# A two-layer conditioned transformer block on one core: a third chunk ahead of the feed-forward stage, a new written order, and more weight splitting on GpSimd

## The reference

```python
# L0: masked attention, RMS norm of its output, shift and scale from cond
q, k, v = (proj(Wq), proj(Wk), proj(Wv))
scores = jnp.where(mask[None, None, :, :], -jnp.inf, scores)
out = einsum('bhst,bhtd->bhsd', softmax(scores, axis=-1), v) @ Wo.T
xn = out / sqrt(mean(out*out) + EPS) * rms_scale
x = x + xn * (1.0 + sc[:, None, :]) + shift[:, None, :]
# L1 (its sum is added to x once more)
x1 = x + attention(tc_rmsnorm(x, t, g1w, g1b, b1w, b1b), Wq, Wk, Wv, Wo)
x = x + x1 + swiglu(tc_rmsnorm(x1, t, g2w, g2b, b2w, b2b), gate_w, hid_w, out_w)
```

## Time and profile before

| | |
|---|---|
| median of 3 runs | 336.03 us |
| profiled execution | 333.88 us |
| its span | 332.1 us |
| PE busy | 317.1 us, 95% |
| DVE busy | 238.8 us, 72% |
| ACT busy | 208.7 us, 63% |
| POOL busy | 171.8 us, 52% |
| granted TensorE clock, mean | 0.995 of full |

### The profile page before, as it was taken

The page is one execution under the profiler, slowest core; times in us unless marked ns, Lnnn a source line. Parts: engine busy times, 40 slices in busy tenths (PEclk is TensorE's granted clock), DMA queues, the critical chain, the costliest instruction groups (busy, mean ns, idle before and its releaser), DMA issues.

```text
span 332.1 us, 12175 instructions
## 1 busy us (share of the span) xinstructions
PE 317.1 (95%) x5152; PEld 299.5 (90%) x5152; DVE 238.8 (72%) x413; ACT 208.7 (63%) x449; POOL 171.8 (52%) x195
## 2 busy tenths in 40 slices
PE   5999679889999999999999999999999999999995
PEld 5878569788899999999999999999999999999995
DVE  3799855988767788698968887698598685255343
ACT  3888747979686855857598575575554653543221
POOL 7073589950352527358474657638527367144231
PEclk9999979999999999999999999999999999999999
DMA  7926642220301030001300030000001000000000
GB/s 244 261 74 196 191 130 66 80 82 4 100 2 35 2 99 2 3 2 35 97 2 34 10 92 1 2 34 2 2 2 34 5 34 0 2 28 6 2 34 32
DMA packets 11238, 17.09 MB, mean 51 GB/s; under 512 B 1328, under 2 KB 5440, under 8 KB 11184
## 3 DMA queue, kind: packets, MB, share of 16 engines
q1 hardware_dynamic: 11008, 15.80, 15.1%
q0 software_dynamic: 176, 0.51, 0.8%
HBM read 14.14 MB, written 2.16 MB: 49 GB/s over the span
## 4 chain that ended last, share of the span: by engine, by line
PE 82%; DVE 7%; issue 3%; DMA 3%; SPq 2%; ACT 1%; POOL 1%; POOLq 0%; DVEq 0%
PE ps L1565 64%; PE ps L1688 5%; PE ps L1670 5%; PE ps L1721 3%; PE ps L1706 3%; PE ps L1753 2%; DMA w_stage<-in_weights 1%; DMA mod_tile<-mod_rows_dram 1%; SPq L309 1%; DVE row_max L1127 1%; PE ps L1658 1%; DVE probs L1135 1%; PE ps L1732 1%; DVE w_lo L1115 1%; DVE in_lo L1122 1%
## 5 line engine op out<-in xcount | busy, mean ns | idle before, releaser
L1565 PE MATMUL ps<-ff_hi,w_hi 128*128 128x256 f32 x256 | 73.9, 289 | 0.0
L1565 PE MATMUL ps<-ff_hi,w_lo 128*128 128x256 f32 x256 | 72.3, 282 | 0.0
L1565 PE MATMUL ps<-ff_lo,w_hi 128*128 128x256 f32 x256 | 72.3, 282 | 0.0
L469 POOL TENSOR_TENSOR h_lo<-w_stage,h_hi 128x512 fp32r<-128x512 f32 x31 | 40.0, 1293 | 44.3 <-ACT h_hi L752 44.2
L1127 DVE TENSOR_REDUCE row_max<-ps 128x8 f32<-128x512 f32 x64 | 41.7, 681 | 15.3 <-PE ps L1670 15.2
L1565 PEld LDWEIGHTS ps<-ff_hi,w_hi 128*128 128x128 f32 x256 | 48.3, 189 | 0.9 <-issue 0.3
L1217 DVE SCALAR_TENSOR_TENSOR w_stage<-w_stage,ps 128x512 f32<-128x512 f32 x32 | 22.0, 686 | 37.1 <-ACT w_stage L745 37.0
L1565 PEld LDWEIGHTS ps<-ff_hi,w_lo 128*128 128x128 f32 x256 | 48.3, 189 | 0.0
L1565 PEld LDWEIGHTS ps<-ff_lo,w_hi 128*128 128x128 f32 x256 | 48.3, 189 | 0.0
L463 POOL TENSOR_TENSOR probs<-probs,inv_row 128x512 f32<-128x512 f32 x32 | 34.0, 1073 | 26.5 <-DVE inv_row L1148 26.3
L689 ACT ACTIVATE probs<-probs 128x512 f32<-128x512 f32 x64 | 39.1, 628 | 8.5 <-DVE probs L1135 8.3
(11 more groups left out here) (111 smaller groups left out, 824.7 us busy)
## 6 DMA issues: line engine op xcount, KB each, us to landing
w_stage<-in_weights SPq DMA_DIRECT2D x20, 256.0 KB, 4.4
mod_tile<-mod_rows_dram SPq DMA_DIRECT2D x32, 128.0 KB, 3.2
x_T<-in_xT SPq DMA_DIRECT2D x8, 256.0 KB, 3.0
x_row<-in_x SPq DMA_DIRECT2D x8, 256.0 KB, 2.8
out<-x SPq DMA_DIRECT2D x7, 256.0 KB, 2.1
x<-in_cond POOLq DMA_DIRECT2D x1, 392.0 KB, 6.3
out<-x SPq DMA_DIRECT2D x2, 128.0 KB, 1.7
x<-in_rows POOLq DMA_DIRECT2D x1, 96.0 KB, 6.3
```

The lines of the kernel that those rows point to most:

```text
L469: pool.tensor_tensor(h_lo[q % 2][:], h_T[q % 2], h_hi[q % 2][:], ALU.subtract)\
L1565: mm = pe.matmul(dst, x, y, start=first and n == 0, stop=last and n == len(terms) - 1, skip_group_check=True)
```

## The change

It rewrites the order lists of all five streams and the bank tables that go with them, and changes five things that can be named:

- `CHAINS` lets layer 0 of a fourth chunk, (3,0), go before layer 1 of the first, (0,1), and keeps that distance.
- `SWAP` goes from 8 to 6: chains 6 and 7 are weighed the second way.
- `HI_POOL` goes from 8 to 4 and `LO_DVE` from 8 to 6: POOL makes the high parts of blocks 4 to 7 in ACT's place, and the low parts of blocks 6 and 7 in DVE's.
- `LOW_DVE = 29`: the low parts of the last three hidden groups, not of the last one alone, are made on DVE.
- `gain_in` has a wait for `input_lo` or `ff_input_lo`, both on the same stream.

```diff
-LO_DVE, HI_POOL, NSTAGE = 8, 8, 5
+LO_DVE, HI_POOL, NSTAGE = 6, 4, 5
 CHAINS = [
-    (0, 0), (1, 0), (2, 0), (0, 1), (3, 0), (1, 1), (4, 0), (2, 1), (5, 0), (3, 1), (6, 0), (4, 1),
-    (7, 0), (5, 1), (6, 1), (7, 1),
+    (0, 0), (1, 0), (2, 0), (3, 0), (0, 1), (4, 0), (1, 1), (5, 0), (2, 1), (6, 0), (3, 1), (7, 0),
+    (4, 1), (5, 1), (6, 1), (7, 1),
 ]
...
-SWAP = 8
+SWAP = 6
...
+LOW_DVE = 29
...
+        def hidden_lo_of(q):
+            return (h_lo_ready, q + 1) if q < LOW_DVE else (h_lo_last, q + 1 - LOW_DVE)
...
             load_w("k0")
             load_xT(0)
-            load_xT(1)
             load_w("q0")
             load_w("v0")
             load_w("o0")
+            load_xT(1)
             load_w("k1")
...
-                wait(dve, h_lo_ready, q - 1)
+                if q >= 2:
+                    dve.wait_ge(*hidden_lo_of(q - 2))
...
-            def last_hidden_lo():
-                q = 4 * NCH - 1
+            def hidden_lo(k, g):
+                q = 4 * k + g
...
-                pe.wait_ge(h_lo_ready, q + 1)
+                pe.wait_ge(*hidden_lo_of(q))
...
-                pe.wait_ge(h_lo_last, 1)
+                pe.wait_ge(*hidden_lo_of(4 * NCH - 1))
```

More of the change, by code:

```diff
@@ L821, in _ @@
             input_hi(5)
-            input_hi(6)
+            squares_of_y(1)
+            output_hi(2)
+            exponentials(3, 2)
+            copy_keys(4)
+            copy_queries(4)
+            exponentials(3, 3)
+            copy_keys(5)
+            squares_of_x(1)
             copy_pT(3, 1, 0)
@@ L1342, in _ @@
-            shift(6, 2)
-            modulate_y(3)
-            shift(6, 3)
-            norm_output(5)
+            shift(6, 0)
+            shift(6, 1)
+            norm_x(4)
+            sums(6, 0)
+            sums(6, 1)
+            gain_in(4)
+            shift(6, 2)
+            shift(6, 3)
+            sums(6, 2)
+            norm_output(5)
+            ff_input_lo(0)
+            sums(6, 3)
+            maximum(7, 0)
+            maximum(7, 1)
+            shift(7, 0)
+            shift(7, 1)
@@ L1386, in _ @@
+            norm_x(5)
             norm_x(6)
[L1387 to L1388 removed]
+            gain_in(5)
+            gain_in(6)
+            ff_input_lo(1)
             maximum(9, 0)
+            maximum(9, 1)
             shift(9, 0)
[L1391 removed]
+            output_lo(8)
+            result(0)
+            maximum(9, 2)
+            maximum(9, 3)
             shift(9, 1)
+            input_lo(11)
+            shift(9, 2)
             sums(9, 0)
             sums(9, 1)
[L1395 removed]
@@ new lines, in _ @@
+            hidden(1, 0)
+            hidden(1, 1)
+            new_x2(2)
+            shift(9, 3)
+            modulate_y(5)
+            sums(9, 3)
+            hidden(1, 2)
+            maximum(10, 0)
+            maximum(10, 1)
+            shift(10, 0)
+            shift(10, 1)
+            norm_x(7)
+            norm_x(8)
+            sums(10, 0)
+            maximum(10, 2)
+            maximum(10, 3)
+            input_lo(12)
+            sums(10, 1)
+            gain_in(7)
+            gain_in(8)
@@ L1484, in _ @@
+            hidden(3, 0)
+            new_x2(4)
+            sums(13, 3)
+            hidden(3, 1)
             modulate_y(7)
-            hidden(3, 1)
             hidden(3, 2)
-            sums(13, 2)
-            sums(13, 3)
+            norm_x(11)
             norm_x(12)
             hidden(3, 3)
+            gain_in(11)
             gain_in(12)
+            input_lo(15)
+            result(3)
+            ff_input_lo(4)
             maximum(14, 0)
@@ L1877, in _ @@
-            hidden_in(0, 2, y_read(4), out_read(5))
-            hidden_in(0, 3)
-            output_product(5, scores_read(6, 3))
-            transpose_probs(6, 0, v_read(6), oT_read(5))
-            transpose_probs(6, 1, out_read(5), gu_read(0, 0))
-            values(7, gu_read(0, 0))
-            scores(7, gu_read(0, 1), pT_read(6, 0, 0), pT_read(6, 0, 1))
-            hidden_out(0, 0, y_read(5))
-            keys(8, pT_read(6, 1, 0))
-            queries(8, scores_read(7, 0))
-            transpose_normed(4, v_read(7))
@@ L1935, in _ @@
+            hidden_in(1, 3)
+            output_product(8, scores_read(9, 1))
+            hidden_in(1, 4, gu_read(1, 0))
+            hidden_in(1, 5)
+            transpose_probs(9, 0, y_read(8), scores_read(9, 2))
+            scores(10, gu_read(1, 1), scores_read(9, 3), y_read(7))
+            values(10, pT_read(9, 0, 0))
+            hidden_out(1, 0, gu_read(1, 2))
             hidden_out(1, 1)
             hidden_out(1, 2)
+            transpose_normed(7, v_read(10))
+            keys(11, pT_read(9, 0, 1))
@@ L1960, in _ @@
+            queries(12, pT_read(10, 0, 0))
+            transpose_probs(10, 1, pT_read(10, 0, 1), acc_read(1))
+            values(11, scores_read(11, 0))
+            output_product(9, scores_read(11, 1))
+            hidden_in(2, 0, q_read(12), pT_read(10, 1, 0))
             hidden_in(2, 1)
-            hidden_in(2, 2, xsT_read(8), scores_read(11, 1))
+            hidden_in(2, 2, scores_read(11, 2), scores_read(11, 3))
             hidden_in(2, 3)
-            keys(13, scores_read(11, 2))
-            scores(12, k_read(12), q_read(12), gu_read(2, 0))
@@ new lines, in _ @@
+            transpose_normed(10, pT_read(12, 0, 0))
+            output_product(11, oT_read(11))
+            weigh_values_T(12, pT_read(12, 1, 1))
+            scores(13, xsT_read(10), pT_read(12, 0, 1), pT_read(12, 1, 0), gu_read(2, 3))
+            values(13, gu_read(2, 3))
+            hidden_out(2, 6)
+            hidden_out(2, 7)
+            output_product(12, oT_read(12))
+            hidden_in(3, 0, scores_read(13, 0), acc_read(2))
+            hidden_in(3, 1)
+            hidden_in(3, 2, scores_read(13, 1), scores_read(13, 2))
```

1167 lines of the change are left out of this document (555 added, 612 removed), and 20 rows, old and new, of tables (GU_BANK, S_BANK, T_BANK).

## The result

The changed kernel took **325.44 us** as the median of 4 runs (324.68 to 326.48), beside 336.18 us for the kernel before on the same chip (335.86 to 338.05). The ratio is 0.967, with a 95% interval from 0.962 to 0.972: 10.7 us faster, where 6.4 were forecast. The two profiled executions are closer together, 333.88 and 326.18 us, 7.7 us apart. In all that follows the medians are over all runs of a kernel, and the ratios compare only runs within 1.5% of the fastest of their kernel.

What follows compares the result with a forecast made beforehand. PE, busy in 95% of the span, was taken as the bound. The terms -0.6 - 4.8 - 1.0 + 2.0 - 1.4 - 0.6 summed to -6.4 us: 327.5 us profiled, 329.6 us median, range 323 to 337.5 us.

Steps and rivals of the forecast that it cites:

- B: Hole from 30 to 50 us: chain-3 filler saves 7.1 us, POOL's split costs DVE 2.3 us by port contention; -4.8 us.
- A: Start: q0, v0 and o0 loaded ahead of the second x_T, the gain partly waited for again; -0.6 us.
- signs named for B: 35 to 50 us: no clock under 0.9; PE over 9 of 10 us from 30 to 50; first bias_in near 45 us.
- C: Stretch from 60 to 70 us: the order puts input_lo further ahead of its keys; -1.0 us, ends 0 and -2.1.
- D: Chains 6 and 7: SWAP adds row sums on DVE and normalise on POOL; +2.0 us, ends 0 and +7.0.
- E: Chains 6 and 7 on PE: SWAP takes 0.69 us of work off each; -1.4 us, far end 0.
- F: Tail: DVE instead of POOL makes the last low parts, removing PE's wait of 0.7 us; -0.6 us.
- Rival 1: 35 to 110 us: ACT and DVE become the pace; at worst 341.6 us; chance 0.13 slower, 0.11 within 1%.
- Rival 2: Port: five early DVE subtractions each wait for a whole POOL subtraction, 6.5 us instead of 2.3; 333.8 us; chance 0.10.
- Rival 3: Everything fits: A and C in full, B without its 2.3 us, D at nothing; -12.4 us, 323.6 us; chance 0.08.
- at nothing: Costed at no effect: four high parts leaving ACT, gain_in's added wait, and store_mods behind u1 in SP's queue.
- I apply the same difference to the median: Median taken as 2.15 us above the profiled execution before (336.03 against 333.88 us), so 327.5 became 329.6 us.

Runs made afterwards that it cites:

- second group: Four kernels made from the kernel before (split alone, new tail, first loads, extra products), on one chip beside the kernel before: 338.56 us median of its 35 runs.
- first group: Changed kernel again (326.15 us), filler taken out, split undone and SWAP = 5, on one chip beside the kernel before: 338.14 us median of its 23 runs.

## Why the prediction was right, and where it was not

The sign, the place and the bound were right; that the sum came so near is in part luck, as B shows. By profiled executions 6.4 us were forecast and 7.7 came; the median was forecast 4.2 us too high (329.6 against 325.44), inside the range.

**A** (-0.6 forecast): the first 10 us gained 1.8 us of busy PE, and 10 to 30 us gave back 0.8, so 1.0 net. The profile of the run that undoes it says 0.6. The kind of forecast, a gain that is partly waited for again, was right.

**B** (-4.8): 3.1 us of idle time and 1.7 us of clock, 4.8 us in sum. The sum was exact and its parts were not. The port contention that was to cost 2.3 us did not come where it was charged. These are the five subtractions ahead of the first maximum, with those of the earlier trace rows to compare:

```profile
9.26 0.92 DVE L1135 TENSOR_TENSOR in_lo<-x_T,in_hi 128x512 fp32r<-128x512 f32 x1 [1.26 <-ACT in_hi L668]
...
11.06 1.88 DVE L1128 TENSOR_TENSOR w_lo<-w_stage,w_hi 128x512 fp32r<-128x512 f32 x3
13.98 0.69 DVE L1135 TENSOR_TENSOR in_lo<-x_T,in_hi 128x512 fp32r<-128x512 f32 x1 [1.04 <-ACT in_hi L668]
```

They took 3.49 us, and five alone take 5 x 0.69 = 3.45. While DVE made the three `w_lo` POOL stood waiting 3.57 us for a block (from 10.66 to 14.23 us). The first maximum did come 1.4 us later (14.59 against 13.20 us), but the first exponential did not (16.50 against 16.61). In place of the contention came 1.54 us of "issue" from 33.94 us on and a wait of 0.53 us for DVE's `probs` ahead of 46.85 us. So the agreement is a cancellation. Of the signs named for B, the clock came true (1.00 in every window of 2 us from 35 to 50). PE over 9 of 10 us held from 40 to 50 us (9.20), not from 30 to 40 (8.46). And `bias_in` was expected near 45 us and ran at 47.98: I had taken the walk to shorten, and it did not.

**C** (-1.0): 50 to 70 us lost 0.4 us of idle time. The wait for `in_lo` is gone and an issue stall of 1.39 us stands there.

**D** (+2.0): from 70 us on idle time rose by 1.0 us, with none of it a wait for `normalise`. The run with `SWAP = 5` shows that the mechanism is real and starts one chain earlier.

**E** (-1.4): PE's busy time fell from 317.14 to 313.62 us, 3.5 us, of which 1.7 are the clock; the rest, 1.8, is near the 1.4 forecast. The records confirm it: 768 matmuls of L1730, 640 of L1745, and 136 fewer in all.

**F** (-0.6): -0.7; the wait for POOL's `h_lo` is gone.

**Rival 1**: from 50 to 110 us PE was idle 2.5 us in sum, half of the 5 named as its sign, and never over 1.3 us in a stretch of ten. **Rival 2**: the five subtractions above exclude it, and so do the means over the kernel, both under the 1.2 us named as its sign:

```profile
L1135 DVE TENSOR_TENSOR in_lo<-x_T,in_hi 128x512 fp32r<-128x512 f32 x8 | 7.7, 963 | 2.3 <-ACT in_hi L668 2.3
L1128 DVE TENSOR_TENSOR w_lo<-w_stage,w_hi 128x512 fp32r<-128x512 f32 x6 | 4.0, 686 | 1.1 <-ACT w_hi L654 1.1
```

The rule of the Trainium skill (SBUF — State Buffer, "SBUF: two separate sides"), that the loser of the lock waits for the other's whole instruction, is not refuted, and where the two engines met the trace agrees with it. `in_lo` took 1.62 us at 75.99 us and 1.34 us at 138.45 us, and both ended 0.54 us after the POOL instruction that they met (`new_x1`, 75.78 to 77.07 us, and `shift_row`, 137.96 to 139.25 us). The eight `in_lo` from `x_T` cost 963 ns in the mean, before 813, but these two meetings are not with the split's work. **Rival 3** (323.6 us) is nearer to the median than the forecast, but not by its terms: in the profiled pair C came to 0.4 us and D to 1.0, and the sum to 7.7, not 12.4.

**Two steps failed.** The first: "at nothing", for the high parts that leave ACT, and the port as the only effect of the split. Undoing the split in the new order costs 8.8 us. It keeps ACT and DVE free early (2.4 us of the walk) and it frees the slots in time (6.7 us of the walk, by POOL's queue), and without it the late walk stops the filler by way of ACT's `squares_of_x(0)` (6.5 us of PE's time). I had costed who does the work and not when the buffer comes free, nor what stands behind the walk. How much of the 8.8 us each of the two is worth stays open, and the run with SP's queue repaired does not settle it, since it made h2 late itself.

The second: "I apply the same difference to the median." The median is not the profiled execution plus a constant. The mean granted clock of each of 35 runs of the kernel before, in the second group:

| mean clock | runs | medians, us |
|---|---|---|
| 0.994 to 0.995 | 10 | 335.1 and 335.7 |
| 0.989 to 0.990 | 7 | 338.9 and 337.5 |
| 0.984 to 0.985 | 8 | 338.6 and 338.9 |
| 0.979 to 0.980 | 6 | 340.8 and 340.0 |
| 0.974 to 0.975 | 3 | 342.6 and 342.8 |

(Medians are given for the lower and the upper value of each pair; one run at 0.843 took 355.33 us.) A step of 0.005 is 0.005 x 332 = 1.7 us, exactly the loss read in the earlier trace rows. From 0.995 to 0.975 the time rises by about 7 us for 4 steps, 1.8 us each (1.7 by the first three rows alone). The profiled execution had one such drop, at 0.995, and was among the quickest; most runs had two to four. In the trace of the kernel with the new tail in the old order, mean clock 0.98, they can be seen:

```profile
40.00:50.00 10.00, 7.41 (x164) 6.52 (x164) 5.13 (x11) 4.07 (x12) 7.33 (x11) 0.66 0.43 125
50.00:60.00 10.00, 9.32 (x119) 9.03 (x120) 4.37 (x7) 6.50 (x18) 9.67 (x11) 0.83 0.19 56
...
70.00:80.00 10.00, 8.99 (x229) 8.53 (x230) 6.79 (x11) 6.42 (x13) 2.69 (x3) 0.83 0.18 56
```

0.34 + 0.17 + 0.17 of 10 us is 6.8 us, four times 1.7, and PE's busy time is 322.7 us there, 5.6 us more than in the profiled kernel before with its one drop (317.1). The changed kernel had a mean clock of 0.999 or 1.000 in all ten of its runs in the result and the first group. So the gain has two parts: 7.7 us in the profiled pair, with one drop in it, and the further drops that most runs of the kernel before had. That the filler is what removes the drops is shown by the run without it, whose clock fell to between 0.979 and 0.990 in all 12 runs.

The drops account for only a part of the missing 3 us. Of these, 0.7 us is the changed kernel, whose median is under its own profiled execution (325.44 and 326.18 us). The other 2.3 us is the kernel before, whose profiled execution was a quick one even for its clock: 333.88 us, where the ten runs at 0.995 in the table have 335.1 and 335.7. In the second group, 4.7 us above the profiled execution by the median, some 3 us are drops and some 1.5 the spread at one clock. What made that spread no run shows, and for the first four runs themselves no clock is on record.

## What to carry to other kernels

When a filler goes into a hole, ask not only who does each piece of work but when the piece frees its buffer, and what stands behind the loads that wait for it: moving weight parts to an idle engine was worth nothing in one order and 8.8 us in the other. Look also for what the filler's own copies stand behind: here one late step ahead of them on ACT stopped the filler for 6.5 us. A short idle hole of PE costs more than its length if the clock falls behind it, and that cost differs from run to run, so read the mean clock of all runs and not of the profiled one alone. An exact sum is no proof of its terms: check each against its own row, as here where a contention that did not come where it was charged was made up by a stall that nobody expected.

## What the runs showed of the hardware

- The clock lost by the kernel before came in equal pieces of 1.7 us, one to five of them in 34 of 35 runs. Eighteen extra products in one hole left pieces in other places (50 to 54 us, 72 to 74 us of the profiled execution), raised the mean clock of its runs only from 0.987 to 0.991 and saved no time.
- With the filler taken out, 10 us at 0.50 of full, in which PE was busy for 4.90 us, came with only 2.1 us more busy time of PE over the kernel: at the lower clock the idle part costs nothing more.
- DVE's subtraction of two SBUF tensors took 0.69 us alone and up to 1.62 us (75.99 us) when a POOL instruction of 1.29 us had begun ahead of it.
- PE can stand idle for up to 1.54 us within a run of small matmuls without any engine having held it up (3.4 us in all at L1730), and for up to 2.1 us (3.5 us in all) at the same code with `SWAP = 5`. Other work placed inside one run removed its stall, and another stall, at L1589, grew from 0.7 to 1.2 us.
